# Attention with scores made once: blocks of 128 queries, keys on partitions, the row maximum taken from the scores' own banks

## What is computed

```
N_HEADS = 8; D_HEAD = 64; SCALE = D_HEAD ** (-0.5)
x = ft.reshape(B, N, C)                       # 16, 1024, 512
qkv = x @ w_qkv + b_qkv
qkv = qkv.reshape(B, N, N_HEADS, 3 * D_HEAD)
q, k, v = jnp.split(qkv, 3, axis=-1)
attn = jnp.einsum('bxhd,byhd->bxyh', q, k) * SCALE
attn = jax.nn.softmax(attn, axis=2)
res = jnp.einsum('bxyh,byhd->bxhd', attn, v)
res = res.reshape(B, N, N_HEADS * D_HEAD)
res = res @ w_out + b_out
res = res + x
```

## Time and profile before

| | us |
|---|---|
| median of 3 runs | 3604.11 |
| runs | 3601.85 to 3605.69 |
| the profiled execution | 3603.24 |
| its span, first to last instruction | 3600.7 |
| mean granted TensorE clock | 0.999 |

### The profile page before, as it was taken

One profiled execution on the slowest core, in us unless ns is written; L12 is line 12 of the kernel. 1 busy time (PEld: TensorE's weight loads), 2 busy tenths in 40 slices (PEclk: granted clock), 3 DMA queues, 4 the chain that ended last, 5 costly groups with the idle time before them and its releaser, 6 DMA issues.

```text
span 3600.7 us, 93452 instructions
## 1 busy us (share of the span) xinstructions
PE 3527.6 (98%) x37132; PEld 2155.3 (60%) x37132; DVE 2689.1 (75%) x4643; ACT 3015.9 (84%) x5142; POOL 1949.6 (54%) x1022
## 2 busy tenths in 40 slices
PE   7999999999999999999999999999999999999998
PEld 4656566665666656666665666656666566665664
DVE  6777777777777777777777777777777777777775
ACT  6888878888788887888878788787888878888786
POOL 2564654556455564565645556455565555656545
PEclk9999999999999999999999999999999999999999
DMA  2011110111102011020110101112011110111101
GB/s 91 12 47 40 47 43 16 54 34 50 42 15 62 28 50 42 14 68 21 49 42 26 60 18 48 43 30 60 16 47 42 43 46 18 47 43 37 45 16 54
DMA packets 100709, 144.70 MB, mean 40 GB/s; under 512 B 16192, under 2 KB 48960, under 8 KB 100288
## 3 DMA queue, kind: packets, MB, share of 16 engines
q1 hardware_dynamic: 100288, 138.74, 13.0%
HBM read 71.57 MB, written 33.55 MB: 29 GB/s over the span
## 4 chain that ended last, share of the span: by engine, by line
PE 84%; ACT 5%; POOL 4%; issue 3%; DVE 2%; DMA 0%; SPq 0%; ACTq 0%; DVEq 0%
PE psum L577 33%; PE psum L596 11%; PE psum L632 10%; PE psum L634 10%; PE psum L659 4%; PE psum L657 4%; PE psum L658 4%; POOL p_lo L493 3%; PE psum L662 3%; ACT p_full L747 2%; ACT p_hi L748 2%; PE psum L586 2%; PE psum L661 1%; POOL xT_lo L487 1%; PE psum L604 1%
## 5 line engine op out<-in xcount | busy, mean ns | idle before, releaser
L493 POOL TENSOR_TENSOR p_lo<-p_full,p_hi 128x1024 f16<-128x1024 f32 x768 | 1635.5, 2130 | 1511.7 <-ACT p_hi L748 1511.7
L852 DVE TENSOR_REDUCE max_parts<-psum 128x1 f32<-128x512 f32 x2048 | 1369.1, 683 | 427.0 <-PE psum L596 425.7
L747 ACT ACTIVATE p_full<-psum,prob_bias 128x512 f32<-128x512 f32 x2048 | 1430.5, 698 | 176.8 <-PE psum L634 152.3
L748 ACT ACTIVATE p_hi<-psum,prob_bias 128x512 f16<-128x512 f32 x2048 | 1431.5, 699 | 0.0
L632 PE MATMUL psum<-q_hi_hi,k_lo_hi 128*128 128x512 f16 x2048 | 777.1, 379 | 18.2 <-ACT p_hi L748 10.3
L634 PE MATMUL psum<-q_shift,k_shift 128*128 128x512 f16 x2048 | 776.2, 379 | 0.0
L657 PE MATMUL psum<-v_parts,p_hi 128*128 128x65 f16 x6144 | 754.3, 192 | 12.0 <-POOL p_lo L493 12.0
L596 PE MATMUL psum<-k_lo_hi,q_hi_hi 128*128 128x512 f16 x2048 | 743.9, 380 | 16.8 <-DMA q_hi_hi<-q_hi_hi 4.7
L658 PE MATMUL psum<-v_parts,p_hi 128*128 128x64 f16 x6144 | 755.1, 193 | 0.0
L659 PE MATMUL psum<-v_parts,p_lo 128*128 128x65 f16 x6144 | 753.0, 194 | 0.0
L657 PEld LDWEIGHTS psum<-v_parts,p_hi 128*128 128x128 f16 x6144 | 585.8, 98 | 136.1 <-issue 22.8
(11 more groups left out here) (72 smaller groups left out, 4894.7 us busy)
## 6 DMA issues: line engine op xcount, KB each, us to landing
y_tile<-in_x SPq DMA_DIRECT2D x125, 256.0 KB, 2.8
result<-y_tile SPq DMA_DIRECT2D x125, 256.0 KB, 2.0
x_in<-in_xT SPq DMA_DIRECT2D x121, 256.0 KB, 2.9
q_hi_hi<-q_hi_hi SPq DMA_DIRECT2D x256, 64.0 KB, 1.9
k_shift<-k_lo_hi SPq DMA_DIRECT2D x256, 64.0 KB, 1.9
o_heads<-in_L_conv_w_qkv SPq DMA_DIRECT2D x12, 256.0 KB, 4.7
p_full<-in_xT SPq DMA_DIRECT2D x4, 256.0 KB, 5.2
o_heads<-in_L_conv_w_out SPq DMA_DIRECT2D x4, 256.0 KB, 3.0
```

The lines of the kernel that those rows point to most:

```text
L493: nc.gpsimd.tensor_tensor(p_lo[:, g % LO_SLOTS, :, :], p_full[:, g % 2, :, :], p_hi[:, g % HI_SLOTS, :, :], ALU.subtract).then_inc(p_lo_re ...
L747: nc.scalar.activation(p_full[:, g % 2, n, :], scores(g, n), ACT.Exp, scale=SCALE / (W_SCALE * W_SCALE), bias=prob_bias[:, :])
L748: nc.scalar.activation(p_hi[:, g % HI_SLOTS, n, :], scores(g, n), ACT.Exp, scale=SCALE / (W_SCALE * W_SCALE), bias=prob_bias[:, :]).then_i ...
L852: nc.vector.reduce_max(max_parts[:, u % 2, q_tile, k_half:k_half + 1], bank(b, w), AX.X).then_inc(done["row_max"], 1)
```

## The change

A slot now handles a block: 128 queries of a head against all 1024 keys, keys on partitions in eight tiles side by side, two banks. A set of two banks is used in turn by even and odd blocks.

1. `raw_scores` makes the scores from high parts and key low parts, eight matmuls of 128 columns, and leaves the sum open.
2. `max_over_tiles` on VectorE reduces the two banks over the eight key tiles, reading with a step of 128 elements, to a 128 x 128 map of maxima.
3. `turn_max` transposes the map (fp32) into the free columns of the value bank, `shift_of_queries` reduces it to one negative maximum per query and writes a diagonal with two TENSOR_SCALARs into 64 rows of `q_shift`. The rows of `k_shift` against it hold a constant.
4. `shifted_scores` adds query low parts and shift to the same banks, eight matmuls of 128 columns.
5. `exponentials` reads them once, 1024 columns, into `p_full`; `probabilities_hi` copies `p_full` in SBUF to fp16 `p_hi`.
6. `block_lo` makes every low part on GpSimd. `values` does 24 matmuls two slots later, and the separate add of L893 is gone.

`fill_plan` spreads each projection over two slots in pieces of three terms, one ahead of the shifted scores and one behind the values. `xT_hi`, `xT_lo` and `v_parts` exist twice, and the values of the next image are made for all eight heads at once (512 columns, group 2). `lo_slot` sets in which slot the low part of a fill is made. Three banks serve the fills. The first and last image keep some projections in one piece.

```diff
+def lo_slot(slot, w):
+    if w[0] == "qk" and slot >= 0 and slot % BATCH_BLOCKS != BATCH_BLOCKS - 5:
+        return slot + (3 if slot % 4 == 3 else 2)
...
+    def over_two_slots(slot, b, w):
+        plan.extend([(slot, 0, b, w, 0, 3), (slot, 1, b, w, 3, 6), (slot + 1, 0, b, w, 6, 9), (slot + 1, 1, b, w, 9, TERMS)])
...
-            def row_max_tile(b, w):
-                _, u, q_tile, k_half = w
...
-                nc.tensor.matmul(bank(b, w), q_hi_hi[:, h % 2, q0:q0 + P],
-                                 k_lo_hi[:, h % 2, k_half * HALF:(k_half + 1) * HALF],
-                                 start=True, stop=True).then_inc(ready["row_max"], 1)
...
+            def raw_scores(n):
+                b, h, t, queries = operands(n)
+                if t == 0:
+                    wait_work(pe, done, b, ("qk", h, 1))
+                if t % Q_TILES == 0:
+                    pe.wait_ge(q_hi_hi_ready[t // Q_TILES], (HEADS * b + h + 1) * 16)
+                wait(pe, exp_done, n + 1 - S_SLOTS)
+                for kt in range(TOKEN_TILES):
+                    keys = slice(kt * P, (kt + 1) * P)
+                    last = nc.tensor.matmul(scores(n)[:, keys], k_lo_hi[:, h % 2, keys], q_hi_hi[:, h % 2, queries],
+                                            start=kt % Q_TILES == 0, stop=False, skip_group_check=True)
+                last.then_inc(raw_scores_ready, 1)
+
+            def turn_max(n):
+                pe.wait_ge(max_map_ready, n + 1)
+                wait(pe, neg_max_ready, n)
+                wait(pe, o_ready, (n - PV_LAG) // UNIT)
+                nc.tensor.transpose(max_turned, max_map[:, n % 2, :], identity[:, :]).then_inc(max_turned_ready, 1)
...
+            for g in SLOTS:
+                if is_block(g):
+                    turn_max(g)
+                if is_block(g + 1):
+                    raw_scores(g + 1)
+                fills(g, 0)
+                if is_block(g):
+                    shifted_scores(g)
+                if is_block(g - PV_LAG):
+                    values(g - PV_LAG)
+                fills(g, 1)
...
+            def exponentials(n):
+                wait(act, p_lo_ready, n - 1)
+                act.wait_ge(scores_ready, n + 1)
+                nc.scalar.activation(p_full[:, n % 2, :], scores(n), ACT.Exp, scale=SCALE / (W_SCALE * W_SCALE),
+                                     bias=prob_bias[:, :]).then_inc(exp_done, 1)
+
+            def probabilities_hi(n):
+                wait(act, pv_done, n + 1 - PROB_SLOTS)
+                act.wait_ge(exp_done, n + 1)
+                nc.scalar.copy(p_hi[:, n % PROB_SLOTS, :], p_full[:, n % 2, :]).then_inc(p_hi_ready, 1)
...
+            def max_over_tiles(n):
+                dve.wait_ge(raw_scores_ready, n + 1)
+                nc.vector.tensor_reduce(max_map[:, n % 2, :], scores(n).rearrange("p (t q) -> p q t", q=P), AX.X,
+                                        ALU.max).then_inc(max_map_ready, 1)
+
+            def shift_of_queries(n):
...
+                nc.vector.tensor_reduce(neg_max[:, n % 2, :], max_turned, AX.X, ALU.max, negate=True).then_inc(neg_max_ready, 1)
+                dve.wait_ge(neg_max_ready, n + 1)
+                for half in range(2):
...
+                    last = nc.vector.tensor_scalar(q_shift[0:DIM, h % 2, begin:begin + DIM], identity[rows, rows],
+                                                   neg_max[rows, n % 2, :], 1 / SHIFT_UNIT, ALU.mult, ALU.mult)
+                last.then_inc(shift_ready, 1)
```

More of the change, by code:

```diff
@@ L169 @@
-FILL_ORDER = [(b, w) for b, (w, first, _, _) in FILL_PIECES if first == 0]
-EMPTIED_AFTER = {"qk": 1.7, "v": 1.0, "project": 1.1, "o_transpose": 0.8}
-def banks_in_turn():
-    banks = {work: RING_BANKS[n % len(RING_BANKS)] for n, work in enumerate(RING_ORDER)}
-    free = dict.fromkeys(FILL_BANKS, -100.0)
-    for b, (w, first, last, c) in FILL_PIECES:
-        if first == 0:
-            banks[b, w] = min(FILL_BANKS, key=lambda k: free[k])
-        free[banks[b, w]] = STEPS * b + c + (EMPTIED_AFTER[w[0]] if last == TERMS else STEPS)
-    return banks
@@ L222 @@
[L222 to L227 removed]
+HEAD_BLOCKS = TOKEN_TILES
+BATCH_BLOCKS = HEADS * HEAD_BLOCKS
+BLOCKS = BATCH * BATCH_BLOCKS
+UNIT = Q_TILES
+UNITS = BATCH_BLOCKS // UNIT
+PV_LAG = 2
+FIRST_SLOT = -11
+END_SLOT = BLOCKS + 12
+X_SLOTS, Y_SLOTS, S_SLOTS, PROB_SLOTS = 3, 3, 2, 3
+W_PARTS, X_PARTS = 4, HALVES * CH_TILES
@@ new lines, in banks_in_turn @@
+def banks_in_turn():
+    complete = {(b, w): slot for slot, b, w in COMPLETED}
+    free, owner, banks, before = dict.fromkeys(FILL_BANKS, FIRST_SLOT - 1), {}, {}, {}
+    begin = {(b, w): slot for slot, _, b, w, first, _ in PLAN if first == 0}
+    for work in BEGUN:
+        bank = min(FILL_BANKS, key=lambda k: free[k])
+        assert free[bank] < begin[work], (work, begin[work], free)
+        if bank in owner:
+            before[work] = owner[bank]
+        banks[work], owner[bank] = bank, work
+        free[bank] = lo_slot(complete[work], work[1])
+    return banks, before
```

725 lines of the change are left out of this document (295 added, 430 removed).

## The result

The changed kernel takes 4486.35 us in the median of four runs (4478.41 to 4493.13), beside 3603.74 for the kernel before (four runs, 3601.85 to 3605.69): a ratio of 1.245, 95% interval 1.2425 to 1.2471. The forecast was 3552, its range 3330 to 3715. It was wrong in sign and far outside its range.

What follows compares the result with a forecast made beforehand. TensorE, 98% busy by issue time, was taken as the bound. Fourteen steady batches of 216.4 us (less 3), batches 0 and 15 (208, 203), 48 ahead, 27 behind, plus 37 and 2.5 gave 3552 us, range 3330 to 3715.

Steps and rivals of the forecast that it cites:

- TensorE's own work: TensorE's matmuls and transposes per slot: 3.02 us against 3.46 before, 450 us less in all if nothing else counted.
- The rival of the loads that show: Stationary operand loads before the 128-column matmuls aren't hidden: 0.66 us more a slot, 4030 us; chance 0.03.
- the rival of the slow map of maxima: VectorE's reduction with 512-byte steps over two banks takes up to 2.5 us instead of 1.24: 4070 us; chance 0.05.
- I take the pair to wait once: The shift's two 64x64 TENSOR_SCALARs on VectorE together wait one time for a running GpSimd instruction, as L871 does.
- the walk: Eight slots followed, each instruction at the later of its engine's and inputs' times: 26.38 us with lock waits.
- plain slots ... the shift at 0.63 finds the port free: Slots without special delays: the low part of the slot before the last ends at 0.3 us, so the shift doesn't wait.
- the lock: VectorE's and GpSimd's SBUF instructions exclude each other; shift waits per eight slots: 0.25 us (key copy), 0.79 (y bias), 0.68 (x part).
- GpSimd gets between the two halves: Rival: a waiting y bias or x part runs between the shift's two TENSOR_SCALARs, 10.7 us a batch, 3710 us; chance 0.27.
- the shift finds the port free: Rival: one-source instructions like the shift's TENSOR_SCALARs don't take the port, so 14 us a batch go, 3347 us; chance 0.22.
- the sum: The forecast's addition of slots, waits, first and last batches and ends: 216.4 us a steady batch, 3552 us in all.
- What would show it: Signs listed for the trace, among them a 216 us batch period, TensorE near 90% busy and a largest wait before shifted scores.
- the second half alone is long: Sign that the forecast is wrong: only the second TENSOR_SCALAR of the shift is lengthened, time then near 3700 us.

Runs made afterwards that it cites:

- the first run: The changed kernel, with both TENSOR_SCALARs of the shift reading the diagonal from PSUM instead of SBUF: 3508.67 us, ratio 0.9736 to the kernel before.

## Why the prediction was wrong

**TensorE's own work** was right. The blocks of the slot are 0.11, 0.44, 0.65, 0.44, 0.73 and 0.65 us at their shortest, beside 0.11, 0.445, 0.65, 0.445, 0.73 and 0.65 predicted. The 128-column matmuls, which no row of before showed, start 0.057 us apart, from eight of them in 0.62 with a last one of 0.22:

```profile
2033.63 0.62 PE L551 MATMUL psum<-q_shift,k_shift 128*128 128x128 f16 x8
```

The Trainium skill's figure of about 81 ns (TensorE: Matmul & The Clock Gate, Back-to-back issue gap) is contradicted by this row. The rival of the loads that show is out, and so is the rival of the slow map of maxima (1.214 us).

**"I take the pair to wait once"** is the step that failed, with two errors in it. The first is the size of the pair and its place. I had 0.41 us from four TENSOR_SCALARs 0.16 apart; it is 0.51 (0.26 apart), and would have ended at 1.14 in the walk instead of 1.04. And in "plain slots ... the shift at 0.63 finds the port free" I looked only at the low part of the slot before the last, which is over by then. The next low part comes at 1.07 in the same walk, 0.03 us behind my pair's end, and I didn't weigh that margin. In each slot behind a unit output my own 0.25 us of delay puts the pair past it. The second error is the value of one wait for the pair. L871 in the earlier trace rows is a single instruction; it has no inner boundary. The pair has one, and GpSimd takes it for 2.13 us. The price predicted for the lock was 14 us a batch. A measured slot is 4.35 us in the mean, 278 us a batch where 216 were predicted; the run with the short low part has 211.3, so the lock costs about 67 us a batch, the lower clock included.

**The rival "GpSimd gets between the two halves"** had the mechanism, with 0.27, and a wrong price: 3710 us. Its reading of the earlier trace rows, that who waits gets the port at the next boundary, is what the traces show on both sides. It let only y biases and x parts slip in, 10.7 us a batch. Of the 313 long second halves 239 took more than 2.0 us, which only a low part lasts. In the run with the y bias shortened nearly all of the loss stayed. Priced with the low part, one caught second half costs 2.1 us and not 1.3, and the point of decision, 3.3 us a batch, is passed with two catches in 64 slots; there were some 20 (313 in 16 batches).

**The lock** itself stands as predicted. The pair reading PSUM loses all its waits. The Trainium skill's lock between VectorE and GpSimd (SBUF — State Buffer, Who interferes with whom), with tensor_scalar among those that can take it, is borne out by L757's 2215 ns beside 252, and the rival "the shift finds the port free" is out for the kernel as it is.

**That rival's number**, 3347 us, can be held against two runs. With the pair in PSUM the time is 3508.7, 162 us more; with the pair in SBUF and the short low part (measured once) it is 3448.7, 102 us more. The 60 us between the two are the longer pair: from the transpose at 1602.24 to the end of the PSUM pair at 1603.46 it takes 1.22 us, the load of the stationary operand starts only behind it, at 1603.51, and the block of three terms ahead of the shifted scores lasts 0.717 us in the median. With the pair in SBUF that block lasts 0.653, where 0.65 was predicted; 0.064 us in 960 such slots are 61 us. So in most slots the predicted chain is hidden, but with nothing to spare where I had 0.1 us.

The rest are terms of the sum. Without the lock it had 202.7 us a batch (216.4 less 13.7); the run with the short low part has 3.302 us a slot, 211.3 a batch, and the PSUM run 3.359 and 215.0. Of the 8.6 us that the sum is too small beside the former, about 1.8 are in the 16 slots whose end waits for a unit output (3.38 in the median, 3.27 predicted), 3.0 in the 48 others (3.08 for 3.02), and the remaining 3.8 in what slots with key copies, output transposes and uneven pieces take beyond that. The expectation of the first run took 3347 over and so failed at its upper end.

**The clock** wasn't in the sum. The granted clock was 0.950, so some 10% of the span, 0.05 / 0.5 x 4481 = 448 us, was at 1.2 GHz. One fall follows the collision of 2017.42 shown above; TensorE's timeline:

```profile
2017.77 0.38 PE L500 MATMUL psum<-wqkv_hi,xT_lo 128*128 128x512 f16 x1
2020.78 0.62 PE L551 MATMUL psum<-q_shift,k_shift 128*128 128x128 f16 x8 [2.63 <-DVE q_shift L757]
...
2022.11 0.62 PE L500 MATMUL psum<-wqkv_hi,xT_hi 128*128 128x512 f16 x1
2022.52 0.63 PE L500 MATMUL psum<-wqkv_lo,xT_hi 128*128 128x512 f16 x1
2022.95 0.63 PE L500 MATMUL psum<-wqkv_hi,xT_lo 128*128 128x512 f16 x1
2023.38 0.42 PE L541 MATMUL psum<-identity,max_map 128*128 128x128 f32 x1
```

TensorE stood 2.63 us, then ran again; the 512-column matmuls behind start 0.43 us apart instead of 0.216. I fitted the lengths of 768 slots of the changed kernel to the pair's waits and to the time at the lower clock, beside a constant for each place in the batch: 0.97 us per microsecond waited and 0.36 per microsecond at 1.2 GHz. The latter is 160 us in all. With both prices the changed kernel's 917 us of waits and 445 us at the lower clock make 1049 us, where 1038 were measured above the run with the short low part; the run with the y bias of 8 columns, which the fit didn't see, has 838 and 259, which make 906, where 898 were measured. That is a fit, not an experiment: no run here held the clock up under the same waits. The runs in PSUM and with the low part put later have clocks of 0.998 and 0.999, so the fall comes with the waits and goes with them.

**"What would show it"** had the right signs. The largest new wait is before the shifted scores, released by the shift; the longest TENSOR_SCALAR is above 1 us beside a median near 0.25, under a running GpSimd instruction; the wait for the unit output is there (53.6 us in 221, 0.24 each). The sign for the rival, "the second half alone is long", is met in 135 pairs; in 178 both are. The period of 216 us and a TensorE busy near 90% are not met: 278 us and 79%.

## What to carry to other kernels

Before a VectorE instruction with SBUF operands is put on the path, lay its start beside the starts and ends of all of GpSimd's instructions in the same period, and count a margin below some tenths of a microsecond as a collision: a miss costs the whole GpSimd instruction, 2.1 us for 0.5 us of work. Two short instructions in a row are not one of their summed length, and each boundary must be priced with the longest thing that can be waiting there. The cheapest cures are to let the small operand be read from PSUM (978 us here, at 0.07 us more per pair) or to make GpSimd start its long instruction behind the critical one, with one semaphore wait (883 us).

## What the runs showed of the hardware

- VectorE and GpSimd take turns at the boundaries of their instructions. A half that had waited 0.2 us or more got the port ahead of a queued GpSimd instruction 224 times of 224 in the changed kernel, and a GpSimd instruction that started during a first half got it ahead of the second 306 times of 306. In the run with the y bias of 8 columns 13 second halves that had started only 0.10 us before such a boundary waited for the next low part as well. The turns are unequal since the lengths are: 0.25 us against 2.13.
- GpSimd isn't slowed by these short instructions: its low parts last 2.129 us in the mean in the changed kernel and 2.130 to 2.134 in the others that make them whole, while VectorE's halves of 0.25 us last up to 2.2. A waiting half ends 0.05 us behind the GpSimd instruction's end.
- A 64x64 TENSOR_SCALAR with its matrix source in PSUM and its per-partition factor and output in SBUF takes 0.28 us instead of 0.25 and doesn't wait for GpSimd: none of the 2048 was above 0.3 us.
- Waits of TensorE of 2 to 3 us, many times over in a kernel that keeps it busy otherwise, went with a granted clock of 0.950 in the mean. Where the halves waited 311 us in sum the clock was 0.995 (42 us at 1.2 GHz), at 520 it was 0.983 (136 us), at 838 it was 0.970 (259 us): the price of a wait isn't constant.
- VectorE reduces 128 x 1024 from PSUM with a step of 512 bytes over two banks in 1.214 us, 1.19 ns per element: no slower than two contiguous reductions of 512 (0.683 each).
